# Queries and keys of a two-layer transformer kernel as two short-significand fp32 parts in place of three bf16 parts

## What is computed

```python
x = x + attn0(layernorm(x))   # causal: q, k = rope(x @ w); softmax(q k^T / sqrt(8)) v; @ w_out
x = x + ffn(layernorm(x))     # 128 -> 512 -> 512 -> 512 -> 128
x = x + attn1(layernorm(x))   # not causal; latent projections (64 wide), rope on q and k
x = x + moe(layernorm(x))     # 8 experts 128 -> 512 -> 128, top 2
```

## Time and profile before

| | us |
|---|---|
| median of 3 runs | 2056.3 (2051.78 to 2062.62) |
| span of the profiled execution | 2074.6 |
| PE busy in it | 1758.1 (85%) |
| DVE busy | 1211.2 (58%) |
| ACT busy | 1042.5 (50%) |
| layer 0: projection to output | 15.8 to 682 |
| layer 1: projection to output | 859 to 1801 |

### The profile page before, as it was taken

One profiled execution on the slowest core, in us unless ns is written; L12 is line 12 of the kernel. 1 busy time (PEld: TensorE's weight loads), 2 busy tenths in 40 slices (PEclk: granted clock), 3 DMA queues, 4 the chain that ended last, 5 costly groups with the idle time before them and its releaser, 6 DMA issues. The chain is left out here.

```text
span 2074.6 us, 34644 instructions
## 1 busy us (share of the span) xinstructions
PE 1758.1 (85%) x9416; PEld 706.4 (34%) x9416; DVE 1211.2 (58%) x2462; ACT 1042.5 (50%) x1970; POOL 115.7 (6%) x449
## 2 busy tenths in 40 slices
PE   4123999999998899745599999999999998769999
PEld 2011333323333444310122222222222222447776
DVE  6212888788842210355588878887888883421111
ACT  2011565666676322220077767776777777423443
POOL 2000000000000000010000000000000000000000
PEclk9555999999999999765599999999999999879999
DMA  5754000000000000166400000000000000000000
GB/s 137 131 105 62 4 2 3 1 2 2 2 1 1 1 0 0 48 117 128 61 2 1 2 3 2 2 3 3 1 2 2 2 1 2 1 21 21 20 20 20
DMA packets 55356, 48.72 MB, mean 23 GB/s; under 512 B 14002, under 2 KB 52223, under 8 KB 54527
## 3 DMA queue, kind: packets, MB, share of 16 engines
q1 hardware_dynamic: 55231, 47.14, 11.4%
HBM read 38.74 MB, written 8.39 MB: 23 GB/s over the span
## 5 line engine op out<-in xcount | busy, mean ns | idle before, releaser
L541 DVE TENSOR_REDUCE maxp<-bank 128x1 f32<-128x512 f32 (+3 forms) x1664 | 989.9, 651 | 270.1 <-PE bank L453 163.5
L526 ACT ACTIVATE ring<-bank 128x512 f32<-128x512 f32 (+3 forms) x1664 | 841.1, 577 | 534.9 <-PE bank L466 370.5
L453 PE MATMUL bank<-Ka,Qa 96*128 (+3 forms) x1664 | 638.8, 392 | 123.5 <-DVEq L532 101.3
L466 PE MATMUL bank<-Qa,Ka 96*128 (+4 forms) x1664 | 597.6, 376 | 119.3 <-DMA Qa<-shift_rows 110.3
L482 PE MATMUL bank<-ring,Vst 128*32 128x512 f32 (+3 forms) x3328 | 423.3, 582 | 0.6 <-ACT ring L526 0.6
L453 PEld LDWEIGHTS bank<-Ka,Qa 96*128 (+1 forms) x1664 | 162.9, 99 | 647.7 <-issue 308.8
L466 PEld LDWEIGHTS bank<-Qa,Ka 96*128 96x128 bf16 (+1 forms) x1664 | 161.5, 99 | 307.3 <-issue 114.3
L647 POOL COPY Vst<-V 128x32 f32 (+1 forms) x416 | 85.3, 209 | 1222.1 <-PE bank L482 1221.5
L1010 DVE SCALAR_TENSOR_TENSOR x<-bank,wts,x 128x128 f32<-128x128 f32 x128 | 36.0, 344 | 197.2 <-PE bank L973 197.2
L998 ACT ACTIVATE Qa<-bank,eb 128x512 f32<-128x512 f32 x128 | 86.3, 687 | 104.7 <-PE bank L964 102.4
L973 PEld LDWEIGHTS bank<-Qa 128*128 128x128 f32 x1024 | 118.1, 192 | 11.5 <-issue 11.5
(11 more groups left out here) (118 smaller groups left out, 671.3 us busy)
## 6 DMA issues: line engine op xcount, KB each, us to landing
Ka<-k_parts SPq DMA_DIRECT2D x24, 384.0 KB
Qa<-q_parts SPq DMA_DIRECT2D x72, 128.0 KB
ring<-in_tables SPq DMA_DIRECT2D x2, 2048.0 KB, 8.6
Qa<-shift_rows SPq DMA_DIRECT2D x256, 1.0 KB
Qa<-in_ew SPq DMA_DIRECT2D x16, 256.0 KB, 2.9
q_parts<-Qa SPq DMA_DIRECT2D x8, 384.0 KB, 6.0
k_parts<-Qa SPq DMA_DIRECT2D x8, 384.0 KB, 6.2
Ka<-in_ones SPq DMA_DIRECT2D x8, 384.0 KB
```

Of the source, the lines that this page charges most:

```text
L453: mm = pe.matmul(bank[:, 0:w], k.Qa[0:ROWS, n, j, t * P:(t + 1) * P], k.Ka[0:ROWS, g * HG + j, a:a + w], start=True, stop=not diagonal)
L466: mm = pe.matmul(bank[:, first:CW], k.Ka[0:ROWS, g * HG + j, kt * P:(kt + 1) * P], k.Qa[0:ROWS, n, j, first:CW], start=True, stop=not diag ...
L526: act.activation(k.probs[:, 4 * (kt % 2) + j, first:CW], score[j][:, first:CW], ACT.Exp, scale=scale).then_inc(probs_ready, 1)
L541: dve.tensor_reduce(k.maxp[:, a // CW, t, j:j + 1], for_max[max_bank(shape_c(c), i)][:, 0:w], AX.X, ALU.max).then_inc(max_read, 1)
```

## The change

A head needs 4 products by 8 dimensions = 32 rows; with two rows for the shift it is held in 64 partitions, and two heads share the 128. A score matmul reads 64 partitions, the halves belong to two heads, and the pair writes two banks.

The layout is no longer made by DMA. After the projection PE multiplies `kb` (k's parts) by 0/1 matrices `sel` (from a constants input, 0.95 MB in all) and DVE and ACT copy two banks each into `K`, adding `ones_col`, which puts the ones of the shift rows in. This takes 8 rounds a layer (L213 to L217, L263, L300 of the new kernel). The queries are built unit by unit within the attention: `Qm` (for maxima) and `Qx` (with the shift, which 8 small matmuls on `shiftM` put in) go through the same banks as the scores and ACT copies them out. The banks are dealt anew: three in turn for scores and query building (`E_BANKS`), two pairs in turn for maxima, one for the values. A reduction on DVE reads a pair, two heads, at once: 832 x 512 columns' worth of pairs instead of 1664 single ones. The shift needs no DMA: DVE writes it into `shiftM`. POOL has no work in the attention; the values are read as nine columns a head (`V9`). Loops are written out in full. A mask on a diagonal block is two matmuls of 64 columns for a half of the array instead of one of 128.

The diff, cut to its core:

```diff
-NPART = 3
-PROD = NPART * NPART * HD
-ROWS = 96
-Q_LAYS, K_LAYS = NPART * NPART + 1, NPART + 1
-PART_BUFS = 4
+NB = H // 2
+HALF = P // 2
+SHIFT_ROW = 32
+E_BANKS = 3
 HID = 512
...
+                sp.dma_start(k.cst[:, :], k.in_consts[:, :]).then_inc(consts_loaded, 16)
+                sp.dma_start(k.ident[:, :], k.in_consts[:, 0:P]).then_inc(consts_loaded, 16)
...
-def lay_out(sp, k, layer, c, w):
-
-    src = k.parts[w][:, :, c * CW:(c + 1) * CW].rearrange("b (d h) s -> b d h s", d=HD)
-    for a in range(NPART):
-        if w == 1:
-            first = a * NPART * HD
-            sp.dma_start(k.Ka[first:first + NPART * HD, :, c * CW:(c + 1) * CW],
-                         src.rearrange("b d h s -> (b d) h s")).then_inc(k.k_laid_out[layer][c], 16)
-            continue
-        for b in range(NPART):
-            first = (a * NPART + b) * HD
-            sp.dma_start(k.Qa[first:first + HD, c * G:(c + 1) * G, :, :].rearrange("d g j s -> d (g j) s"),
-                         src[a]).then_inc(k.q_laid_out[layer][c], 16)
...
+            for r, (c, parity) in enumerate(rounds):
+                pe.wait_ge(hi_ready, 2 * c + 2)
+                pe.wait_ge(lo_ready, 2 * c + 2)
+                if r >= 2:
+                    pe.wait_ge(k_built_dve, r - 1)
+                    pe.wait_ge(k_built_act, r - 1)
+                for part, kind in enumerate((SEL_KHI, SEL_KLO)):
+                    for q in range(4):
+                        rows = slice(32 * q, 32 * q + 32)
+                        mm = pe.matmul(k.bank[4 * (r % 2) + q], k.sel[rows, kind, parity, :],
+                                       k.kb[rows, part, c * CW:(c + 1) * CW], start=(part == 0), stop=(part == 1))
+                mm.then_inc(k_psum, 1)
...
+                dve.wait_ge(k_psum, r + 1)
+                dve.tensor_scalar(built(r, 0), k.banks[:, 4 * (r % 2):4 * (r % 2) + 2, :], k.ones_col[:, 0:1], None, ALU.add
+                                  ).then_inc(k_built_dve, 1)
...
+        ebank = lambda e: k.bank[e % E_BANKS]
+        mpair = lambda m: k.banks[:, 3 + 2 * (m % 2):5 + 2 * (m % 2), :]
...
+            def plain_queries(n, b, e):
+                c, g = units[n]
+                rows = slice(32 * g, 32 * g + 32)
+                wait_bank(e)
+                pe.matmul(ebank(e), k.sel[rows, SEL_QHI, b, :], k.qb[rows, 0, c * CW:(c + 1) * CW], start=True, stop=False)
+                return pe.matmul(ebank(e), k.sel[rows, SEL_QLO, b, :], k.qb[rows, 1, c * CW:(c + 1) * CW],
+                                 start=False, stop=True)
+
+            def build_qm(n):
+                for b in (0, 1):
+                    plain_queries(n, b, qm_job(n, b)).then_inc(e_ready, 1)
+
+            def build_qx(n):
+                pe.wait_ge(shift_ready, n + 1)
+                for b in (0, 1):
+                    e = qx_job(n, b)
+                    plain_queries(n, b, e)
+                    for t in range(TC):
+                        mm = pe.matmul(ebank(e)[:, t * P:(t + 1) * P], k.shiftM[:, b, t, :], k.identr[:, :],
+                                       start=False, stop=True, skip_group_check=True)
+                    mm.then_inc(e_ready, 1)
+
...
+                for q, b in enumerate(blocks):
+                    for half in (0, 1):
+                        rows = slice(HALF * half, HALF * half + HALF)
+                        out = mpair(m)[:, half, q * w:(q + 1) * w]
+                        mm = pe.matmul(out, k.Qm[rows, n % 2, b, t * P:(t + 1) * P],
+                                       k.K[rows, 2 * g + b, a * CW:a * CW + w], start=True, stop=True)
...
-                mm = pe.matmul(bank[:, 0:w], k.Qa[0:ROWS, n, j, t * P:(t + 1) * P],
-                               k.Ka[0:ROWS, g * HG + j, a:a + w], start=True, stop=not diagonal)
...
+                mm = pe.matmul(ebank(e)[:, first:CW], k.K[rows, 2 * g + b, kt * P:(kt + 1) * P],
+                               k.Qx[rows, n % 2, b, first:CW], start=True, stop=True)
...
-                mm = pe.matmul(bank[:, first:CW], k.Ka[0:ROWS, g * HG + j, kt * P:(kt + 1) * P],
-                               k.Qa[0:ROWS, n, j, first:CW], start=True, stop=not diagonal)
...
+                for kt in range(steps[n]):
                     for j in range(HG):
-                        scores(c, g, kt, j)
-                        if j < HG - 1:
-                            some_maxima(HG * kt + j)
+                        scores(n, kt, j)
+                        if j == 1:
+                            some_maxima(2 * kt)
+                    if kt == 0 and n + 2 < NU:
+                        build_qm(n + 2)
+                    if kt == qx_after[n] and n + 1 < NU:
+                        while done[0] < urgent:
+                            score_maxima(*todo[done[0]])
+                            done[0] += 1
+                        build_qx(n + 1)
+                    some_maxima(2 * kt + 1)
...
+            def take_queries(dst, e):
+                act.wait_ge(e_ready, e + 1)
+                act.activation(dst, ebank(e), ACT.Copy).then_inc(e_done, 1)
...
+                if len(blocks) == 2:
+                    src = mpair(m)[:, :, 0:2 * w].rearrange("p i (b w) -> p i b w", b=2)
+                    dst = k.maxp[:, n % 2, a, t, :].rearrange("p (b i) -> p i b", i=2)
+                else:
+                    src, dst = mpair(m)[:, :, 0:w], k.maxp[:, n % 2, a, t, 2 * blocks[0]:2 * blocks[0] + 2]
+                dve.tensor_reduce(dst, src, AX.X, ALU.max).then_inc(m_done, 1)
...
-                dve.tensor_reduce(k.maxp[:, a // CW, t, j:j + 1], for_max[max_bank(shape_c(c), i)][:, 0:w], AX.X, ALU.max
...
+            def shift_high(n):
+                dve.wait_ge(neg_ready, n + 1)
+                if n:
+                    dve.wait_ge(e_ready, qx_job(n - 1, 1) + 1)
+                dve.tensor_copy(rows_of(0), by_block(n)).then_inc(hi_ready, 1)
+
+            def shift_low(n):
+                dve.wait_ge(hi_ready, n + 1)
...
-                sp.dma_start(k.shift_dram[:, :], k.shiftT[:, :]).then_inc(shift_stored, 16)
-                sp.wait_ge(shift_stored, 16 * n + 32)
-                for r in range(2):
-
-                    src = k.shift_dram.rearrange("(b c) (t q) -> c t b q", b=4, t=TC)[r * HG:(r + 1) * HG]
-                    for j in range(HG):
-                        sp.dma_start(k.Qa[PROD + r:PROD + r + 1, n, j, :].rearrange("o (t b q) -> o t b q", t=TC, b=4),
-                                     src[j:j + 1]).then_inc(shift_rows, 16)
-            for n in range(2):
```

More of the change, by code:

```diff
@@ L16 @@
 F32 = mybir.dt.float32
+F32R = mybir.dt.float32r
 BF16 = mybir.dt.bfloat16
@@ L343, in _ @@
                         latents(c + 1)
-            second_part(len(items) - 1)
+            for r in range(len(rounds)):
+                act.wait_ge(k_psum, r + 1)
+                act.activation(built(r, 2), k.banks[:, 4 * (r % 2) + 2:4 * (r % 2) + 4, :], ACT.Identity,
+                               bias=k.ones_col[:, 0:1]).then_inc(k_built_act, 1)
 def attention_phase(nc, k, layer):
@@ L378, in piece0 @@
-    def piece0(c, g):
-        if not causal:
-            return (c * G + g) * len(pieces(0))
-        return sum(G * len(pieces(i)) for i in range(c)) + g * len(pieces(c))
-    FREE = 4
-    def max_bank(c, i):
-        return 1 if len(pieces(c)) % 3 == 1 and i == len(pieces(c)) - 1 else i % 3
-    def pieces_back(c, before, i):
-        row = [max_bank(before, n) for n in range(len(pieces(before)))] + [max_bank(c, n) for n in range(i)]
-        return row[::-1].index(max_bank(c, i)) + 1
+    units = [(c, g) for c in range(C) for g in range(G)]
@@ L1058, in build @@
[L1058 to L1066 removed]
+        k.negm, k.maxp = sb("negm", [P, 2, TC, HG]), sb("maxp", [P, 2, C, TC, HG])
```

655 lines of the change are left out of this document (292 added, 363 removed).

## The result

| | median us (lowest to highest) | profiled span | mean granted clock |
|---|---|---|---|
| before | 2059.5 (2051.78 to 2065.26) | 2074.6 | 0.904 |
| after | 2115.8 (2111.12 to 2123.04) | 2121.1 | 0.866 |

The ratio is 1.0275, with a 95% interval of 1.0234 to 1.0317. The forecast was 1890 us, with a range from 1820 to 2090.

The account below looks back on a forecast made before the run. PE was taken to set the steady attention's pace, the operand layout's DMAs to hold up the starts. Terms -28 - 61 - 36 + 5 - 32 - 20 = -172 gave 1903 profiled, x 0.991 = 1886, stated as 1890 us; range 1820 to 2090.

Parts of the forecast that it names:

- Items 1, 5 and 6: Ahead of attention, layer 0 -28 us and layer 1 -32, DMA layout gone; layer 1's first maxima, now paired, -20.
- Item 2: Layer 0's first four units: the shift's DMA and its queue go, 87 us in place of 148, -61.
- Item 3: Layer 1's steady units: three-bank loop takes a step from 2.89 to 2.64 us, layer from 748 to 712, -36.
- (a): Loop links in the steady step: next score to its exponential 0.38 + 0.03 us, within a step of 2.64.
- (b): Query building's cost in each attention unit, partly in the ring: 2.3 us, between 0 and 4.3.
- (c): Layer 1's units, all sixteen priced alike, the last included: 44.5 us each.
- Item 4: Layer 0's other twelve units (424 us): wide-step gain against queries and more masks, +5, between -30 and +60.
- the sum of -24 and +28: Layer 0's other twelve units: 96 wide steps gain 0.25 us each, -24; query building adds 28.
- The upper end, +60: Layer 0's other twelve units, if pieces under 256 columns run at the fp32 price, 0.2 to 0.4 us each.
- B: Rival for the attention's matmuls: one column a clock but halves not abreast, step 2.97, 2010 us; chance 0.14.
- C: Rival for the attention's matmuls: an F32R column takes two clocks, step 3.30, 2170 us; chance 0.15.
- D: Rival for the wide steps: PE granted less clock, a third of them slow costs 160, 2044 us; chance 0.06.

Follow-up runs that it names:

- noquery: Changed kernel with queries built only for the first two units of each layer, later units reusing them; 0.9432 of the kernel before.
- bf16ops: Changed kernel with K, Qm and Qx stored as bf16 instead of F32R, same instructions; 0.9499 of the kernel before, 1954 us.
- the fillers: Changed kernel plus two unread matmuls a step in each layer's last unit, and one PE wait; 1.0086 (64 rows) and 1.0121 (128 rows) of the kernel before.
- mfirst: Changed kernel with each step's second pair of maxima moved ahead of the last score; 0.988 of the kernel before, 2034 us.
- nomask: Changed kernel without the causal masks' matmuls, for scores and maxima; 1.0205 of the kernel before.
- singles: Changed kernel with paired maxima undone: four score banks, three single maxima banks, one reduction for each bank; 1.0108 of the kernel before.
- wide0: Changed kernel with each step's first score, behind the values, taken over all 128 rows; 1.034 of the kernel before.

## Why the prediction was wrong, point by point

The forecast span was 1903 us and the measured one 2121: 218 us.

- **Items 1, 5 and 6 held** (-37, -33 and -19 where -28, -32 and -20 stood). That the first rotation would move to 24.6 was wrong: it stands at 20.56, and the attention starts at 53.4. From there to the first copy into K it took 21.3 us, not 26.5, and K's rounds took 11.1, not 10.
- **Item 2: the mechanism held, the size didn't**, 114 us instead of 87. `noquery` has 90 there: the building of queries, costed at nothing in these four short units, is 24 of the 27 missing. The type weighs there too (95 us in `bf16ops`); the two overlap and can't be added.
- **Item 3 is the step that failed**, in three terms, 140 us. (a) "The next score's pass and drain 0.38 + 0.03" was read from bf16 rows with a covered weight load; with F32R and the load in the open it is 0.59, and the last score with its maxima 0.65, not 0.59. The step is 2.86, not 2.64: 0.22 x 16 = 3.5 us a unit, 53 us over fifteen units. `bf16ops` shows the loop, and its sum, right for bf16, two of its links by errors that cancel. (b) "I take 2.3 (between 0 and 4.3)" for the queries: the unit has 5.3 outside its steps, 3.0 more, 45 us; `noquery` prices them at 51.1 - 46.3 = 4.8, of which a low-clock stretch is 1.1 to 1.6. (c) The last unit at the low clock took 65.1 and not 44.5, 21 us. Another 21 are units longer than 51.1, in which longer low-clock stretches fall (15 units took 787.2, 15 x 51.1 is 766.5).
- **Item 4**: +66 where +5 stood. `noquery` has 430 there and `bf16ops` 426, so the masks (8 us, where the sum of -24 and +28 leaves 1 for them) aren't it, and the same two terms with the clock (0.86) are. The two kernels overlap, as both also raise the clock (0.93, 0.94), so the three can't be added up. The upper end, +60, rested on pieces "under 256 columns" at the fp32 price. No run shows such a threshold, and the scores on a diagonal block speak against the price. At the full clock the first mask starts 0.34 us behind its score of 512 columns and 0.17 behind one of 128; the 384 columns between take 0.17 us, and one column a clock would be 0.16:

```profile
583.94 0.51 PE L419 MATMUL banks<-Qx,K 64*128 64x512 f32 x2
584.28 0.24 PE L424 MATMUL banks<-ident,mask_exp 64*128 64x64 bf16 x4
...
594.33 0.33 PE L419 MATMUL banks<-Qx,K 64*128 64x128 f32 x2
594.50 0.24 PE L424 MATMUL banks<-ident,mask_exp 64*128 64x64 bf16 x4
```

- **Rivals.** B and C fell: the halves run abreast, and F32R takes one column a clock at 512 columns (starts 0.23 apart). D, the granted clock, was given 0.06, and it happened in part; its row ("was never granted more", at 70% busy) was read and then set aside for a stretch of another stage. The low clock took about 570 us of the span against about 400 before. Its price, 160 us, is not borne out. In the last two units the fillers gave back 40 us. By the earlier trace rows and the changed kernel's rows by stage, the other units had about 130 us more at the low clock than before; at `noquery`'s 1.1 to 1.6 us for each 3.4, that is an estimate of 40 to 60 us.
- **The chances.** "Slower" got 0.20 although the forecast gain rested on reading a new operand's latency from another type's rows. I had bounded the F32R matmul's throughput from both sides, but not its latency from start to reader. In a loop through three banks it is the latency that counts.

What stays open: why the last unit falls to 1.2 GHz and stays there in the changed kernel, `mfirst` and `nomask`, and not in `noquery`, `bf16ops`, `singles` or `wide0`, which add no filler. In layer 1 `noquery` does the same 192 matmuls at 1.00 with PE busy 82%, the changed kernel at 0.50 with 92%; at the low clock each matmul lasts longer, so the higher share is in part an effect. Open are also what the wait ahead of the last unit does without the fillers, and the last 0.02 to 0.04 of each F32R link, beyond its weight load.

## What to carry to other kernels

When a new order turns a gap-free engine into a loop over few banks, cost the loop with the new operands' latencies, weight loads included: here about 0.1 us at two places a step, 0.22 together, was more than the 0.19 that a step was to gain (2.83 before, 2.64 forecast). Ask of each instruction in the loop whether it must stand there; moving one pair of maxima gave back 4%. Give a price to the work that takes a DMA's place inside the loop: building the queries, with the low-clock stretch that came with it, cost 4.8 us of a unit's 51.1.

## What the runs showed of the hardware

- An F32R weight load of 128 columns takes 0.18 to 0.19 us over 32, 64 or 128 rows, a bf16 one 0.09 to 0.10.
- Two matmuls on the two row halves start about 0.01 us apart and run abreast, with F32R as with bf16.
- The last unit of layer 1, the same 192 matmuls, ran at 0.50 for 61 of its 65.1 us in one kernel and at 1.00 in another (42.6 us). Two filler matmuls a step, with one wait ahead of the unit, kept the clock up (0.92 to 1.00) and saved 19 to 21 us in such a unit over 64 rows, 14 to 15 over 128.
- F32R scores of 128 and of 512 columns differ by 0.17 us from their start to the next matmul, which is about one column a clock.
- A VectorE maximum over two banks of 512 columns starts every 1.13 us, one over a single bank every 0.60.
